# Second FFN of a gated block: activations turned through DRAM, gated values widened by ScalarE, other PSUM banks

## The chip, the cores and the metric

The kernel runs on one core of a Trainium2 chip. A core has TensorE (matmuls and transposes, results in PSUM, eight banks of 2 KB per partition), VectorE, ScalarE and GpSimd for the rest, SyncE that issues transfers, and 16 DMA engines. The engines run side by side, each its own list in order; semaphores are all that ties one list to another. The metric is the device time in microseconds of the whole program.

## The reference

x has 8 batches of 256 rows of 512, that is 16 tiles of 128 rows. Four sublayers are added to x one after the other; the last, the second FFN, is what the change touches:

```python
x = x + tanh(g_xattn[0]) * L0_xattn(ctx, ctx, layernorm(x), ...)
x = x + tanh(g_ffn[0])   * L0_ffn(layernorm(x), ...)
x = x + tanh(g_xattn[1]) * L1_xattn(layernorm(x), ctx, ...)
x = x + tanh(g_ffn[1])   * L1_ffn(layernorm(x), w1, g1, w2, g2, w3, g3)

def _rmsnorm(x, g):  return g * (x * rsqrt(mean(x * x, axis=-1) + 1e-8))
def _act_quant(x):
    scale = 127.0 / clip(max(abs(x), axis=-1), 0.0001)
    return clip(round(x * scale), -128, 127) / scale
def _linear_bit(x, w, g): return _act_quant(_rmsnorm(x, g)) @ _ternary_quant(w).T

def _L1_ffn_ref(x, w1, g1, w2, g2, w3, g3):      # 512 -> 2048 -> 512
    h = silu(_linear_bit(x, w1, g1)) * _linear_bit(x, w2, g2)
    return _linear_bit(h, w3, g3)
```

## The kernel before

A tile t of 128 rows goes through the second FFN in these steps. Its values are small integers after quantisation, kept as bf16.

1. `x_stats` (VectorE, L1685): mean and variance of the row. `x_norm` (GpSimd, L564): four small operations give the factor of LayerNorm and RMS norm together.
2. `x_gain` (VectorE, L1691): (x - mean) * g, once for g1 and once for g2, into `xg`. `x_max`, `x_scales` (L1697, L1701): the largest value and the scales.
3. `x_quant` (ScalarE, L904): int16 into `qi4`. `x_widen` (VectorE, L1711): bf16 into `qb4`.
4. `x_T` (TensorE, L1163): eight 128 by 128 transposes into PSUM bank 2. `x_out` (ScalarE, L922): copy to `xq4T`.
5. `up` (TensorE, L1255): four chunks c of 512 columns. Each is two groups of four matmuls, with w1 into bank 3 + c % 2 and with w2 into bank 5 + c % 2. A chunk waits until `gate` has read the chunk two before it.
6. `silu` (ScalarE, L926) reads the first bank into `sil`, `gate` (VectorE, L1766) multiplies the second bank, its scale and `sil` into `hh`, and counts `h_done`.
7. `h_gain` (GpSimd, L576): hh * g3 into `hg`, 512 columns at a time. `h_max` (VectorE, L1773): the largest of each. `h_squares` (ScalarE, L943): sums of squares over chunks 0 to 2, then 3. `h_rms` (GpSimd, L580) and `h_scales` (VectorE, L1778): the scales.
8. `h_quant` (ScalarE, L931): int16 in two halves. `h_widen` (VectorE, L1790): bf16 into `hqb`, in two halves.
9. `hidden_T` (TensorE, L1264): sixteen transposes into banks 0 and 1. `h_out` (ScalarE, L937): copies to `hqT`.
10. `down` (TensorE, L1272): sixteen matmuls with w3 into bank 7. `finish` (VectorE, L1796): scale and add to `x_res`; SyncE stores the tile (L430).

Every engine has a `ffn_body(t, ...)` in which it does its part of several tiles. In body t, tile t goes through steps 5 to 7 (its scales come in body t+1), tile t-1 through steps 8 to 10, tile t+1 through steps 2 to 4. `finish(t-2)` opens VectorE's body. TensorE's body is `up(t)` chunks 0 to 2, `hidden_T(t-1)`, chunk 3, twelve matmuls of `down(t-1)`, `x_T(t+1)`, the last four. The order within a list is written by hand.

The last two attention bodies (`attn_body(NB - 2)` and `attn_body(NB - 1)`, with NB = 8) prepare tiles 0 and 1, and the end of the last attention batch (`latent_ln(7)`, `relu(7)`, `out_proj(7)`, `attn_end(7)`) lies inside body 0. After body 15 come `finish(14)`, `h_scales(15)`, the widening, `hidden_T(15)`, `down(15)` and `finish(15)`.

## Time and profile before

| | |
|---|---|
| median of 3 runs | 741.81 us (741.56 to 744.07) |
| profiled execution | 739.38 us, its span 737.6 us |
| TensorE matmul, busy over the span | 650.4 us, 88% |
| VectorE | 597.9 us, 81% |
| ScalarE | 493.7 us, 67% |
| GpSimd | 331.7 us, 45% |
| mean granted TensorE clock | 0.970 |
| second FFN, first `up` to the last `finish` | 517.3 to 734.9 us |

Busy time of matmuls runs from start to modelled end of each, and they are pipelined, so it is more than the work. Durations are of one profiled execution. An idle time before an instruction is put down to the engine, or the DMA, whose signal came last. A letter q behind an engine's name (SPq, PEq) means its queue of issues. The span lacks what lies before the first and after the last instruction, 1.8 us here.

### The profile page before, as it was taken

How to read it: one execution, taken by the hardware profiler on the slowest of the kernel's cores; microseconds unless marked ns; L12 is line 12 of the kernel's file. 1: busy time of each engine (PE TensorE's matmuls, PEld its weight loads, DVE VectorE, ACT ScalarE, POOL GpSimd, SP SyncE). 2: the span in 40 equal slices, each digit the busy share in tenths (PEclk: the TensorE clock that was granted, in tenths of full speed). 3: DMA queues.
4: the chain of work that ended last, by engine and by line, in shares of the span. 5: the costliest groups of instructions: out<-in, count | busy, mean ns of one | idle time of the engine just before them, and what ended most of it. 6: DMA issues, size and time to landing. Idle time of an engine off the chain costs nothing.

```text
span 737.6 us, 10458 instructions
## 1 busy us (share of the span) xinstructions
PE 650.4 (88%) x3211; PEld 385.5 (52%) x3211; DVE 597.9 (81%) x1114; ACT 493.7 (67%) x743; POOL 331.7 (45%) x420
## 2 busy tenths in 40 slices
...
DMA packets 73135, 87.38 MB, mean 118 GB/s; under 512 B 36672, under 2 KB 43600, under 8 KB 71952
## 3 DMA queue, kind: packets, MB, share of 16 engines
...
q8 instruction: 14, 0.23, 0.1%
...
## 4 chain that ended last, share of the span: by engine, by line
PE 30%; DVE 22%; issue 22%; ACT 16%; POOL 6%; DMA 3%; DVEq 0%; POOLq 0%; SPq 0%; ACTq 0%
PE ps L1027 16%; PE ps L1133 4%; PE ps L1097 4%; ACT arena L948 4%; DVE arena L1694 3%; DVE q L1699 2%; ACT turn L843 2%; ACT arena L797 2%; DVE arena L1769 2%; ACT turn L908 2%; DMA arena<-kpad_d 1%; DVE arena L1794 1%; PE ps L1278 1%; DMA arena<-in_x 1%; ACT arena L924 1%
## 5 line engine op out<-in xcount | busy, mean ns | idle before, releaser
L1027 PE MATMUL ps<-arena 128*128 128x288 f32 x640 | 159.8, 411 | 6.6 <-POOL arena L492 3.0
L1027 PEld LDWEIGHTS ps<-arena 128*128 128x128 f32 x640 | 121.7, 192 | 41.8 <-issue 7.6
L1260 PE MATMUL ps<-arena 128*128 128x512 bf16 x512 | 116.2, 380 | 9.1 <-ACT arena L924 7.6
L578 POOL TENSOR_TENSOR arena<-arena 128x512 f32<-128x512 f32 x64 | 87.8, 1374 | 68.9 <-DVE arena L1769 68.8
L1260 PEld LDWEIGHTS ps<-arena 128*128 128x128 bf16 x512 | 47.5, 98 | 71.4 <-issue 14.2
L1133 PE MATMUL ps<-arena 128*128 128x512 bf16 x256 | 60.8, 403 | 9.3 <-DVE arena L1583 6.7
L491 POOL TENSOR_TENSOR arena<-arena 128x1024 f32<-128x1024 f32 x32 | 60.6, 1894 | 13.0 <-ACT arena L672 7.5
L1410 DVE TENSOR_TENSOR turn<-ps,arena 128x768 f32<-128x768 f32 x32 | 30.6, 957 | 39.0 <-PE ps L1027 27.2
L1278 PE MATMUL ps<-arena 128*128 128x512 bf16 x256 | 61.9, 387 | 0.1
L1097 PE MATMUL ps<-arena 128*128 128x512 bf16 (+1 forms) x256 | 57.5, 382 | 1.8 <-ACT arena L797 1.7
L498 POOL TENSOR_TENSOR turn<-turn 128x512 f32<-128x512 f32 x32 | 42.5, 1327 | 26.1 <-DVE turn L1420 26.0
L928 ACT ACTIVATE arena<-ps,q 128x512 f32<-128x512 f32 x64 | 41.7, 674 | 16.5 <-PE ps L1260 16.5
L685 ACT ACTIVATE arena<-arena 128x512 f32<-128x512 f32 x32 | 19.9, 626 | 43.9 <-DVE turn L1420 43.9
L1133 PEld LDWEIGHTS ps<-arena 128*128 128x128 bf16 x256 | 26.1, 103 | 43.7 <-issue 17.3
L1769 DVE SCALAR_TENSOR_TENSOR arena<-ps,q,arena 128x512 f32<-128x512 f32 x64 | 47.5, 744 | 0.7 <-ACT arena L928 0.5
L797 ACT ACTIVATE arena<-ps,b,s 128x512 f32<-128x512 f32 x64 | 45.0, 795 | 3.6 <-PE ps L1097 2.7
L1775 DVE TENSOR_REDUCE q<-arena 128x1 f32<-128x512 f32 x64 | 42.0, 676 | 1.7 <-POOL arena L578 1.6
L934 ACT ACTIVATE arena<-arena,q 128x1024 int16<-128x1024 f32 x32 | 35.0, 1141 | 12.3 <-DVE q L1788 12.3
L1504 DVE TENSOR_REDUCE hmax<-arena 128x1 f32<-128x2048 f32 x15 | 34.0, 2277 | 9.2 <-ACT arena L797 9.2
L1097 PEld LDWEIGHTS ps<-arena 128*128 128x128 bf16 x256 | 24.7, 99 | 32.0 <-ACT arena L797 3.1
L1420 DVE TENSOR_TENSOR turn<-ps,turn 128x1024 f32<-128x1024 f32 x32 | 39.2, 1225 | 1.1
L1278 PEld LDWEIGHTS ps<-arena 128*128 128x128 bf16 x256 | 24.8, 99 | 28.2 <-issue 2.4
...
## 6 DMA issues: line engine op xcount, KB each, us to landing
...
tern_d<-late SPq DMA_DIRECT2D x24, 256.0 KB, 6.1
arena<-in_x SPq DMA_DIRECT2D x4, 1024.0 KB, 9.6
arena<-in_ctx SPq DMA_DIRECT2D x4, 1024.0 KB, 17.4
...
x_d<-arena SPq DMA_DIRECT2D x4, 1024.0 KB, 4.2
arena<-x_d SPq DMA_DIRECT2D x4, 1024.0 KB, 7.7
```

Source lines behind the costliest of these rows:

```text
L491: pool.tensor_tensor(dst[:, :, 0:32].rearrange("p r (d i) -> p r d i", d=4), a, shifted, ALU.mult)
L498: po.done(pool.tensor_tensor(x[:, :, 0:16], x[:, :, 0:16], x[:, :, 16:32], ALU.add))
L578: pool.tensor_tensor(hg[:, s, sl], hh[:, s, sl], g3[:, sl], ALU.mult).then_inc(S["hg_done"], 1)
L797: act.activation(hid[:, q, f, :], ps[:, f % 4, :], ACT.Gelu, bias=b1[:, f:f + 1], scale=s1[:, f:f + 1]).then_inc(S["gelu_done"], 1)
L928: act.activation(sil[:, c, :], ps[:, 3 + c % 2, :], ACT.Silu, scale=q4[:, 11 + 2 * s:12 + 2 * s]).then_inc(S["sil_done"], 1)
L1027: last = pe.matmul(ps[:, 4 * s + lo, 0:NB * PAIRS], toep[:, u, (LB - 1 - lo + li) * P:(LB - lo + li) * P], kv[:, s, li, :], start=(li == 0 ...
L1097: last = pe.matmul(ps[:, f % 4, :], fw1T[:, k, f * P:(f + 1) * P], xqT[:, k, ds(L * r, L)], start=(k == 0), stop=(k == LB - 1))
L1133: return pe.matmul(ps[:, 2 * j + f // 8, :], hq[:, r % 2, f, j * P:(j + 1) * P], fw2T[:, f, :], start=(f % 8 == 0), stop=(f % 8 == 7))
L1260: last = pe.matmul(ps[:, 3 + 2 * j + c % 2, :], xq4T[:, s, 4 * j + k, :], w[:, k, c * L:(c + 1) * L], start=(k == 0), stop=(k == LB - 1))
L1278: last = pe.matmul(ps[:, 7, :], hqT[:, f, :], bw3T[:, f, :], start=(f == 0), stop=(f == FT - 1))
L1769: v.scalar_tensor_tensor(out=hh[:, s, c * L:(c + 1) * L], in0=ps[:, 5 + c % 2, :], scalar=q4[:, 12 + 2 * s:13 + 2 * s], in1=sil[:, c, :], ...
L1775: dv.done(v.tensor_reduce(q4[:, 32 + c:33 + c], hg[:, s, c * L:(c + 1) * L], AX, ALU.max, apply_absolute_value=True))
```

## The change

Its parts, by engine:

- SyncE: `x_turned(t)` stores `qb4` (256 KB) to DRAM, waits until it has landed, and reads it back transposed into `xq4T`. `h_turned(t)` does so with `hqb` (512 KB) into `hqT`, which now has two places. Both stand in SyncE's list with the stores of the result: for each t, `h_turned(t-1)`, `store(t-2)`, `x_turned(t+2)`.
- TensorE: `x_T` is gone. `hidden_T` is there for tile 15 alone. `up` writes three pairs of banks, (3, 5), (4, 6), (0, 1) and (3, 5) again; chunk 0 waits for the last gate of the tile before, chunk 3 for the tile's first gate. `down(t-2)` is in body t, in two pieces around `up(t, 3)`, into bank 7 or 2 by turns.
- ScalarE: `x_out` is gone, `h_out` is there for tile 15 alone. It gets `h_widen` (one pass of 2,048 columns after both halves of `h_quant`) and `x_centre` (mean - x into `xc`).
- GpSimd: gets `x_gain`, one product of 1,024 columns of `xc`, repeated, with g1 and g2; for tiles 0 and 1 `x_centre` as well. `h_rms(t-1)`, `x_norm(t+2)` and `x_gain(t+2)` stand before the four `h_gain(t)`.
- VectorE: `x_gain` and `h_widen` are gone, `h_max` works on halves of 1,024 columns. `finish(t-2)` stands between `h_max(t, 0)` and `gate(t, 3)`.
- Tile x is prepared two bodies ahead instead of one.

```diff
@@ SyncE
+            def x_turned(t, s, past):
+                sp.wait_ge(S["qb_ready"], t + 1)
+                if past is not None:
+                    sp.wait_ge(xT_in[s], 16 * past)
+                sp.dma_start(xq_d[s], qb4).then_inc(S["xq_stored"], 16)
+                sp.wait_ge(S["xq_stored"], 16 * t + 16)
+                if past is not None:
+                    sp.wait_ge(S["upb_done"], 4 * t - 4)
+                sp.dma_start_transpose(xq4T[:, s], xq_d[s]).then_inc(xT_in[s], 16)
+            def h_turned(t, s, past):
+                sp.wait_ge(S["hqb_ready"], 2 * t + 2)
+                if past is not None:
+                    sp.wait_ge(hT_in[s], 16 * past)
+                sp.dma_start(hq_d[s], hqb).then_inc(S["hq_stored"], 16)
+                sp.wait_ge(S["hq_stored"], 16 * t + 16)
+                if past is not None:
+                    sp.wait_ge(S["dn_done"], t - 1)
+                sp.dma_start_transpose(hqT[:, s], hq_d[s]).then_inc(hT_in[s], 16)
+            x_turned(0, 0, None)
+            x_turned(1, 1, None)
+            x_turned(2, 0, 1)
+            for t in range(1, NT):
+                h_turned(t - 1, (t - 1) % 2, (t - 1) // 2 or None)
+                if t >= 2:
+                    store(t - 2)
+                if t + 2 < NT:
+                    x_turned(t + 2, t % 2, t // 2 + 1)
@@ GpSimd
+            def x_gain(t):
+                pool.wait_ge(S["xc_ready"], t + 1)
+                pool.tensor_tensor(xg[:, :, :], xc.unsqueeze(1).to_broadcast([P, 2, L]), g12[:, :, :],
+                                   ALU.mult).then_inc(S["xg_ready"], 1)
+            def ffn_body(t, s, nxt2):
+                h_rms(t - 1)
+                if nxt2:
+                    x_norm(t + 2)
+                    x_gain(t + 2)
+                for c in range(4):
+                    h_gain(t, s, c)
+            x_norm(0)
+            x_centre(0)
+            x_gain(0)
             latent_norm(NB - 2)
-            pool.wait_ge(S["gs_in"], 48)
             x_norm(1)
+            x_centre(1)
+            x_gain(1)
+            x_norm(2)
+            x_gain(2)
             latent_norm(NB - 1)
@@ ScalarE
+            def x_centre(t):
+                act.wait_ge(S["st4"], t + 1)
+                act.wait_ge(S["xg_ready"], t)
+                act.activation(xc, x_res[:, ds(t, 1), :].rearrange("p a l -> p (a l)"), ACT.Identity, scale=-1.0,
+                               bias=mv[:, 0, 0:1]).then_inc(S["xc_ready"], 1)
+            def h_widen(t):
+                act.wait_ge(S["hqi3_ready"], 2 * t + 2)
+                if not isinstance(t, int) or t >= 1:
+                    act.wait_ge(S["hq_stored"], 16 * t)
+                act.activation(hqb, hqi, ACT.Copy).then_inc(S["hqb_ready"], 2)
+            def ffn_body(t, s, nxt2, prev):
+                if nxt2:
+                    x_centre(t + 2)
                 silu(t, s, 0)
+                silu(t, s, 1)
                 if prev:
-                    h_quant(t - 1, 1 - s)
-                silu(t, s, 1)
+                    h_quant(t - 1, 1 - s % 2)
                 silu(t, s, 2)
                 if prev:
-                    h_out(t - 1)
-                if nxt:
-                    x_quant(t + 1)
+                    h_widen(t - 1)
+                if nxt2:
+                    x_quant(t + 2)
                 if not prev:
                     relu(NB - 1)
                 silu(t, s, 3)
@@ TensorE
             def up(t, s, chunks):
                 for c in chunks:
-                    pe.wait_ge(S["h_done"], 4 * t + c + 1)
+                    if isinstance(t, int) and t == 0:
+                        if c >= 2:
+                            pe.wait_ge(S["h_done"], c + 1)
+                    elif c == 0:
+                        pe.wait_ge(S["h_done"], 4 * t + 2)
+                    elif c == 2 and isinstance(t, int):
+                        pe.wait_ge(S["x3_done"], 6 + 2 * NB)
+                    elif c == 3:
+                        pe.wait_ge(S["h_done"], 4 * t + 3)
+            def ffn_body(t, s, pair):
+                pe.wait_ge(xT_in[s], 16 * pair + 16)
                 up(t, s, (0, 1, 2))
+                pe.wait_ge(hT_in[s], 16 * pair)
+                down(t - 2, s, 0, 8)
                 up(t, s, (3,))
+                down(t - 2, s, 8, FT)
@@ VectorE
             def attn_body(b, p, nxt, nxt2, prev):
                 if nxt and not nxt2:
-                    v.wait_ge(S["gs_in"], 48)
                     x_stats(0)
-                    x_gain(0)
-                    x_max(0)
+                if not nxt:
+                    x_max(1)
+                    x_scales(1, 1)
+                    x_stats(2)
...
                 if nxt and not nxt2:
+                    x_max(0)
                     x_scales(0, 0)
...
+            def ffn_body(t, s, nxt2, nxt3, prev, prev2):
+                u = s % 2
                 if prev:
+                    h_max(t - 1, 1 - u, 1)
+                    h_scales(t - 1, 1 - u)
                 gate(t, s, 0)
                 gate(t, s, 1)
                 if not prev:
                     latent_ln(NB - 1)
+                if nxt2:
+                    x_max(t + 2)
                 gate(t, s, 2)
+                if nxt2:
+                    x_scales(t + 2, (s + 2) % 4)
+                h_max(t, u, 0)
+                if prev2:
+                    finish(t - 2, u)
                 gate(t, s, 3)
+                if nxt2:
+                    x_widen(t + 2)
                 if not prev:
                     attn_end(NB - 1)
+                if nxt3:
+                    x_stats(t + 3)
```

## Rows read from the trace of the kernel before

**Rows 1.** Busy time of the engines in two stretches of the second FFN.

```profile
core 0: us, PE busy (x) PEld busy (x) DVE busy (x) ACT busy (x) POOL busy (x), PEclk, DMA share, GB/s
544.40:712.30 167.90, 157.92 (x936) 76.28 (x936) 161.99 (x349) 141.06 (x196) 97.09 (x144) 1.00 0.05 20
...
712.30:737.60 25.30, 17.98 (x96) 8.29 (x96) 11.91 (x26) 13.43 (x18) 6.76 (x10) 0.93 0.09 32
```

**Rows 2.** The chain that ended last, bodies 2 to 14, by line.

```profile
by line: issue 20.2%; ACT arena L948 16.0%; DVE arena L1694 12.8%; DVE q L1699 8.8%; DVE arena L1769 6.1%; ACT turn L908 5.8%; DVE arena L1794 4.6%; ACT arena L928 4.4%; POOL q L587 4.3%; ACT arena L924 4.3%; DVE q L1704 1.8%; DVE q L1783 1
```

**Rows 3.** Timeline of bodies 8 and 9: start us, duration us, engine, line, operation.

```profile
624.27 2.19 ACT L934 ACTIVATE arena<-arena,q 128x1024 int16<-128x1024 f32 x2 [0.51 <-DVE q L1788]
...
625.04 1.71 POOL L578 TENSOR_TENSOR arena<-arena 128x512 f32<-128x512 f32 x1 [0.28 <-DVE arena L1769]
...
627.22 0.75 DVE L1794 CAST arena<-arena 128x1024 bf16<-128x1024 int16 x2
...
628.35 1.94 ACT L940 ACTIVATE arena<-ps 128x1024 bf16<-128x1024 bf16 x2 [0.74 <-PE ps L1268]
...
628.68 1.90 PE L1260 MATMUL ps<-arena 128*128 128x512 bf16 x8
...
634.94 5.35 PE L1260 MATMUL ps<-arena 128*128 128x512 bf16 x24 [0.46 <-ACT arena L924]
```

**Rows 4.** Groups of instructions: ns min/median/max, or busy us and mean ns.

```profile
L578 POOL TENSOR_TENSOR arena<-arena x64: 1266/1271/1720, 522.9 to 721.5; 128x512 f32<-128x512 f32 x64
...
L491 POOL TENSOR_TENSOR arena<-arena 128x1024 f32<-128x1024 f32 x32 | 60.6, 1894 | 13.0 <-ACT arena L672 7.5
...
L928 ACT ACTIVATE arena<-ps,q 128x512 f32<-128x512 f32 x52 | 33.7, 673 | 7.8 <-PE ps L1260 7.8
...
L908 ACT ACTIVATE turn<-arena,q 128x512 int16<-128x512 f32 x26 | 17.4, 714 | 3.1 <-DVE q L1709 3.1
...
L948 ACT ACTIVATE arena<-arena 128x512 f32<-128x512 f32 x14 | 8.7, 620 | 0.0
...
L886 ACT ACTIVATE arena<-arena x12 | 23.0, 1916 | 0.0
...
L928 ACT ACT_TABLE_LOAD x1 | 1.3, 1283 | 0.0
...
L1694 DVE SCALAR_TENSOR_TENSOR arena<-arena,mv x32: 740/748/1765, 493.4 to 702.9; 128x512 f32<-128x512 f32 x32
...
L1699 DVE TENSOR_REDUCE q<-arena x16: 1201/1202/1220, 494.9 to 705.9; 128x2 f32<-128x1024 f32 x16
```

**Rows 5.** DMAs: one line's issues and landings, then KB and median landing.

```profile
L416 SPq DMA_TRANSPOSE arena<-tern_d x12: 1972/2365/4210, 368.3 to 398.8; - x12
...
DMA to landing us min/median/max: 4.4/4.9/8.0
...
x_d<-arena SPq DMA_DIRECT2D x4, 1024.0 KB, 4.2
...
out_x<-arena SPq DMA_DIRECT2D x16, 256.0 KB, 2.0
```

**Rows 6.** Timeline of the way into the second FFN.

```profile
508.60 0.19 POOL L551 TENSOR_TENSOR sm<-eps_ln,sm 128x1 f32<-128x1 f32 x1 [13.05 <-DVE sm L1662]
...
515.75 0.70 DVE L1649 BATCH_NORM_STATS2 bn<-ps 128x6 f32<-128x512 f32 x1 [1.96 <-PE ps L1226]
...
527.30 0.74 DVE L1769 SCALAR_TENSOR_TENSOR arena<-ps,q,arena 128x512 f32<-128x512 f32 x1
...
544.45 1.25 PE L1260 MATMUL ps<-arena 128*128 128x512 bf16 x5 [0.52 <-ACT arena L924]
```

**Rows 7.** Timeline of the end.

```profile
720.13 3.62 PE L1278 MATMUL ps<-arena 128*128 128x512 bf16 x16
...
723.79 0.75 DVE L1799 SCALAR_TENSOR_TENSOR arena<-ps,q,arena 128x512 f32<-128x512 f32 x1 [0.26 <-PE ps L1278]
...
728.80 5.31 PE L1278 MATMUL ps<-arena 128*128 128x512 bf16 x16
```

More of the change, by code:

```diff
@@ L219, in flamingo_gated_block @@
         q4 = sb("q4", [P, 36])
+        up_scale = sb("up_scale", [P, 4, 2])
         ps = ctx.enter_context(nc.psum_tensor("ps", [P, 8, 512], F32))
@@ L253, in flamingo_gated_block @@
         c_in = [sem(f"c_in{g}") for g in range(NG)]
+        xT_in = [sem(f"xT_in{s}") for s in range(2)]
+        hT_in = [sem(f"hT_in{s}") for s in range(2)]
         block = ctx.enter_context(nc.Block())
@@ L602, in _ @@
                 h_gain(0, 0, c)
-            h_rms(0)
-            with po.loop(NT // 2 - 1, 10) as i:
+            ffn_body(1, 1, True)
+            with po.loop(NT // 2 - 2, 2 * 5) as i:
                 for u in range(2):
-                    ffn_body(2 * i + 1 + u, (1 + u) % 2, True)
+                    ffn_body(2 * i + 2 + u, u, True)
+            ffn_body(NT - 2, 0, False)
             ffn_body(NT - 1, 1, False)
+            h_rms(NT - 1)
         @block.scalar
@@ L963, in ffn_body @@
                 silu(t, s, 3)
-                h_squares(t, s, 0)
-                if nxt:
-                    x_out(t + 1, 1 - s)
-                h_squares(t, s, 1)
-            x_out(0, 0)
-            ffn_body(0, 0, True, False)
-            with act.Fori(0, NT // 2 - 1) as i:
-                for u in range(2):
-                    ffn_body(2 * i + 1 + u, (1 + u) % 2, True, True)
-            ffn_body(NT - 1, 1, False, True)
+                h_squares(t, s % 2, 0)
+                h_squares(t, s % 2, 1)
+            x_quant(1)
+            ffn_body(0, 0, True, False)
+            ffn_body(1, 1, True, True)
+            with act.Fori(0, 3) as i:
+                for u in range(4):
+                    ffn_body(4 * i + 2 + u, (2 + u) % 4, True, True)
+            ffn_body(NT - 2, 2, False, True)
+            ffn_body(NT - 1, 3, False, True)
             h_quant(NT - 1, 1)
-            h_out(NT - 1)
+            h_widen(NT - 1)
+            h_out()
         @block.tensor
@@ L1160, in _ @@
             pe.wait_ge(S["w3_out"], 1)
-            def x_T(t):
-                pe.wait_ge(S["qb_ready"], t + 1)
-                for n in range(8):
-                    last = pe.transpose(bank_bf(2)[:, n * P:(n + 1) * P], qb4[:, n * P:(n + 1) * P], identb[:, :])
-                last.then_inc(S["xT_tr"], 1)
             def project(b, p):
@@ L1270, in hidden_T, with down @@
                     last.then_inc(S["hT_tr"], 1)
-            def down(t, first, end):
-                if first % 8 == 0:
-                    pe.wait_ge(S["hT_out"], 2 * t + first // 8 + 1)
+            def down(t, s, first, end):
                 if first == 0:
@@ L1685, in x_stats @@
             def x_stats(t):
+                if not isinstance(t, int) or t >= 1:
+                    v.wait_ge(S["xg_ready"], t)
                 dv.done(v.bn_stats(bn[:, 0, :], x_res[:, ds(t, 1), :].rearrange("p a l -> p (a l)")))
```

154 lines of the change are left out of this document (61 added, 93 removed).

## The prediction

> **What bounds the kernel now.** I read the stretches first, then the chain, then one body of the second FFN in order of time. The FFN's 16 tiles take 218 of 737.6 us. From 544.4 (start of body 2) to 712.3 (start of body 15) 13 bodies take 167.9 us, 12.92 each, and VectorE is busy for 161.99/13 = 12.46 of it; TensorE's 12.15 is not its work, since pipelined matmuls count long [rows 1]. Of its real work: 24 matmuls show 5.35 us (634.94) and 8 show 1.90 (628.68) [rows 3], so one costs (5.35 - 1.90)/16 = 0.216 us, and the 48 of a body (32 up, 16 down) 10.35; the last one ends 0.39 after its start. The chain of a body goes through VectorE's `x_gain` (L1694), `x_max`, ScalarE's squares and `x_out` [rows 2]. It closes on itself: tile t+1 is centred, scaled, quantised, turned and projected inside body t.
>
> **VectorE and ScalarE in a body.** VectorE loses `x_gain`, a pair of 0.75 and 1.77 = 2.5 us, and `h_widen`, 0.75; `h_max` becomes two reduces of 1,024 at 1.20 [rows 3, 4]. 12.46 - 3.25 leaves 9.2 busy [rows 1]. ScalarE loses `h_out`, 1.94 [rows 3], and `x_out`, half of that by its form; it gets `h_widen`, the form of L886 (2,048 int16 to bf16), 1.92, and `x_centre`, a 512 pass like the squares' 0.62 [rows 4]: 10.85 - 2.9 + 2.5 = 10.5 busy [rows 1].
>
> **GpSimd in a body.** It gets `x_gain`, 1,024 products. Bounds: 1.89 from L491 (1,024 columns, one operand repeated) and 2.55 from two of L578 [rows 4]. I take 2.4, nearer to L578, whose operands are as large. `h_gain` stays 1.27 and loses its 1.71 case, which lies beside `x_gain` on VectorE [rows 3, 4]. Of its 97.09/13 = 7.47 [rows 1] the four gains are 3 x 1.27 + 1.71 [rows 3, 4], so the norm and root chains 2.0, with their gaps 2.4. The new sum is 5.1 + 2.4 + 2.4 = 9.9.
>
> **The new body.** Time 0 is when TensorE starts `up(t, 0)`. TensorE then has no wait inside the body: `down(t-2)` stands between, and three pairs of banks leave only `up(t, 3)` waiting for `gate(t, 0)`. It ends its 48 matmuls at 10.35. Three loops must be weighed:
> - TensorE and VectorE. VectorE's list is ..., `gate(2)`, `x_scales`, `h_max(0)`, `finish(t-2)`, `gate(t, 3)`. `finish(t-2)` waits for `dn_done`, the last matmul of body t, and `up(t+1, 0)` waits for `gate(t, 3)`. So both lie between two bodies of TensorE. From the last matmul's start: 0.39 to its end, 0.04 to `finish` (723.75 to 723.79), 0.75 for it, the same for the gate, 0.05 to TensorE; less the 0.216 slot already counted [rows 3, 7]. That is 1.77, and the body is 10.35 + 1.77 = 12.1.
> - GpSimd. From the end of `gate(t-1, 3)`: `h_gain` to 1.35, `h_rms` and `x_norm` to 3.75, `x_gain` to 6.15, `h_gain` 0 and 1 to 8.65, then on VectorE `h_max(0)` 1.2, `finish` and `gate` 1.5: 11.4. With 1.89 for `x_gain` it is 10.9, with 2.55 it is 11.5; all hidden. It decides only if GpSimd's part is 0.7 longer.
> - ScalarE. `x_max` ends at 7.3, `gate(2)` 8.0, `x_scales` 8.6, `x_quant` (two of 0.71) 10.0, `silu(3)` (0.67) 10.7, then the gate: 11.4 [rows 4].
>
> I take the first, 12.1. 13 bodies: 167.9 - 157.3 = **10.6 saved**.
>
> **The turns through DRAM.** `h_quant(t-1)` starts at 3.6 (after `silu(1)` and the scales), `h_widen` ends at 8.2. SyncE then waits and issues (0.2), stores 512 KB, waits, and issues the transpose. The store is bounded by 2.0 (256 KB) and 4.2 (1,024 KB), by size 2.7. The transpose of 512 KB landed in 4.4 to 8.0, median 4.9, with up to 12 behind one another [rows 5]. So it lands at 8.2 + 0.2 + 2.7 + 0.1 + 4.5 = 15.7, and `down(t-1)` wants it in the next body at 12.1 + 5.2 = 17.3: 1.6 of cover. If that is gone each us late is a us per body. Behind it on SyncE's queue stand `store(t-2)` and `x_turned(t+2)`; the queue is free again at about 18, the next `hqb` comes at 20.3, and x has 4 us of cover. TensorE is rid of 24 transposes a body, a gain that counts for nothing while it waits 1.77.
>
> **The way in.** `x_centre(1)` and `x_gain(1)` now follow `latent_norm(6)` on GpSimd (508.60 before), and VectorE's `x_max(1)`, `x_scales(1)`, `x_stats(2)` stand before `latent_stats(7)`, which began at 515.75 after an idle 1.96 [rows 6]. Before that, `x_max(0)` behind GpSimd moves the last attention body by 0.8 to 1.4. Then 509.7 + 0.8 + 1.35 + 0.6 + 2.4 = 514.9, and 1.2 + 0.6 + 0.9 give 517.6 for `latent_stats(7)`. In body 0 `x_max(2)` stands before `gate(0, 2)`, and ScalarE's `x_quant(2)` before `relu(7)`, on which `out_proj(7)` hangs: `gate(0, 3)`, begun at 527.30 [rows 6], would end at 532.6 instead of 528.04. `up(1)` has no `down` with it, so half of this comes back. Following body 1 (`attn_end`, four passes at 0.7, statistics 0.9, `h_max`, scales, GpSimd's norm and gain 3.7, `x_max`, gate, scales, reduce, gate), body 2 starts at 546.8 instead of 544.45. I take **+2.4**, between 1.9 and 2.9 by the same steps with the bounds of each.
>
> **The way out.** B is the start of `up(15, 0)`. Before, the last `finish` starts at B + 21.83 (712.33 to 728.80 + 5.31 + 0.04). After, `down(14)` waits for h(14), B + 15.7. TensorE has then been idle 5.4 us; in the last `down` before, after gaps, 16 matmuls took 5.31 instead of 3.62, its first half spaced 0.43 (the 1.2 GHz level; the granted mean of that stretch is 0.93) [rows 1, 7]. So `down(14)` ends at about B + 21.0. h(15): `gate(15, 3)` ends at 12.0, `h_gain` 13.4, `h_max` and scales 15.6, `h_quant` 17.8, `h_widen` in one piece 19.7, so `hidden_T(15)` stands behind `down(14)`: 21.0, then 1.7 to the first half's copy, 3.25 for 15 matmul slots, 0.42 to `finish`: 26.4. **+4.6**; 2.9 if the clock holds in `down(14)`, 5.5 if it doesn't return for `down(15)`.
>
> **Sum.** -10.6 + 2.4 + 4.6 = -3.6 on a span of 737.6. The profiled execution took 739.38 (1.8 around the span), the median 741.81 is 2.4 above that; both are kept. 741.8 - 3.6 = **738.2**. By the bounds: -10.6 + 1.9 + 2.9 = -5.8, and with a body of 12.3, -8.0 + 2.9 + 5.5 = +0.4: its own range is 736.0 to 742.2.
>
> **Rivals.**
> - A, the order costs nothing: TensorE's end and the gate don't form a loop, and GpSimd and ScalarE at 11.4 bind. 13 x 0.7 = 9.1 less: 729.1. For it: nothing but that I may misread a wait. 0.06.
> - B, GpSimd's and VectorE's loop binds: the longest and shortest of L578 (1.27, 1.72) and of L1694 (0.74, 1.77) show [rows 4] that products of two SBUF operands on the two engines disturb each other. For it: only 0.7 of cover and a dozen handovers in that loop. Against: no two-operand SBUF product is left on VectorE in the body. Body 12.6: 13 x 0.5 = +6.5: 744.7. 0.15.
> - C, the slower side: h lands late. It costs from a landing above 6.1 us, and above 6.9 the body is longer than before. At 8.0, the row's maximum: 8.2 + 3.0 + 8.0 - 5.2 = 14.0 per body, +14.2 + 2.4 + 8.1 at the end = +24.7: 766; at 6.9 it is 12.9, and 2.4 + 7.0 for the two ends: 751. Against: the 8.0 had other transposes ahead of it, here at most one of x, with pauses. 0.13.
> - E, the same place at its extreme: the 16 blocks of h are turned one after another. Twelve transposes of 16 blocks each were issued from 368.3 to 398.8, 2.8 us each [rows 5], so a block takes at most 0.17 to 0.28 us of a landing, and this is excluded: 0. By the Trainium skill (VectorE: DVE Perf Modes, The three transpose paths and Rules for kernel authors) a 128 by 128 transpose takes 1309 ns by DMA and 390 on TensorE, which it advises when the result may go to PSUM; sixteen in series would be 20.9 us and a body of about 27, and the trace does not agree that they run in series.
> - D, ScalarE reloads its tables between `x_centre` (Identity) and Silu, 1.28 each, two per body [rows 4]: ScalarE's 10.5 becomes 13.1, and so does the body: 13 x 0.2 + 7.0 = +9.6: 751. No row has the two functions side by side. By the Trainium skill (ScalarE: Activation LUTs, Table sets: the hidden batching unit) identity is in every set, which speaks against it. 0.03.
>
> The forecast keeps 0.63.
>
> **Range and chances.** 0.5% is 3.7 us, about what a measurement can tell here, so the bounds are 738.1 and 745.5. The forecast lies on the first. Faster: 0.32 of the forecast + 0.06 = 0.38. Same: 0.31 + 0.08 of B = 0.39. Slower: 0.07 + 0.13 + 0.03 = 0.23. Range 730 to 750: it leaves out half of A, two thirds of C, and D.
>
> **What would show it.** After the change: body 12.1; on TensorE one gap of 1.8 per body, ended by the gate's line, and VectorE waiting about 0.5 for `down` before `finish`; no wait of TensorE for a DMA in bodies 3 to 15; `x_gain` on GpSimd at 2.4; transposes landing by 5 us; body 2 at 547; 26 us from `up(15, 0)` to the last `finish`, with a gap of 5 before `down(14)`. Wrong if a `down` waits on the DMA, if the gap of TensorE is ended by ScalarE or GpSimd's work, or if `finish` finds `dn_done` already there.

## The result, and the profile after

| | before | after |
|---|---|---|
| median (range) | 742.94 us (741.56 to 745.91) | 757.97 us (755.97 to 760.32), 4 runs each |
| ratio | | 1.0204, 95% interval 1.0168 to 1.0239 |
| profiled execution, its span | 739.38, 737.6 us | 755.97, 754.1 us |
| mean granted TensorE clock | 0.970 | 0.946 |
| x_stats(0) to body 2 | 492.49 to 544.45: 51.96 us | 495.01 to 553.80: 58.79 us |
| bodies 2 to 14 | 167.87 us | 170.64 us |
| up(15, 0) to the last finish | 21.84 us | 26.48 us |

The change made the kernel 15 us slower; 3.6 us faster was forecast. The forecast of the end held (+4.6), the one of the way in was 4.4 too small, and the bodies got 2.8 us longer instead of 10.6 shorter. Another 2.5 us stand ahead of `x_stats(0)`, the first instruction in the table: the profiled executions are 16.6 us apart, and the four stretches are 2.5, 6.8, 2.8 and 4.6. The twelve kernels below have the changed kernel's code up to there; eleven reach `x_stats(0)` at 493.8 to 496.6 and one at 499.8, so it moves by several us without a change of code. How much of the 2.5 belongs to the change stays open.

The stretches that answer [rows 1], in the same columns, and two more that show the clock:

```profile
core 0: us, PE busy (x) PEld busy (x) DVE busy (x) ACT busy (x) POOL busy (x), PEclk, DMA share, GB/s
553.80:724.40 170.60, 144.63 (x611) 61.95 (x624) 135.30 (x265) 135.62 (x181) 118.62 (x151) 0.95 0.48 139
724.40:750.90 26.50, 21.34 (x94) 9.28 (x96) 9.35 (x19) 15.46 (x18) 8.09 (x11) 0.87 0.31 89
...
585.00:632.00 47.00, 38.95 (x176) 17.10 (x177) 38.77 (x73) 39.06 (x51) 33.27 (x40) 1.00 0.47 135
632.30:635.70 3.40, 3.36 (x8) 1.16 (x9) 2.91 (x10) 2.65 (x6) 2.95 (x8) 0.50 1.01 290
```

VectorE did get its relief, 10.4 us busy a body instead of 12.5, and GpSimd is at 9.1 instead of 7.5. Neither is full, and the body is still not shorter. From one `up(t, 0)` to the next the 13 bodies take, in us:

```
13.83 12.71 13.83 12.72 12.73 12.72 13.80 12.72 13.72 12.71 12.71 12.72 13.73
```

There are two lengths. Eight bodies take 12.72. Five take 1.0 to 1.1 more, and each of these has 3.4 us at a granted clock of 0.50, the 1.2 GHz level (in the first it is the second half of a fall of 6.8 us that began before the body). Before, the whole stretch was at 1.00 [rows 1]. Eight times 12.72 and five times 13.8 are the 170.6.

Where 12.72 comes from is read in one body at full clock, the answer to [rows 3]: timeline, start us, duration us, engine, line, operation, and what ended the idle time before it.

```profile
646.14 5.35 PE L1334 MATMUL ps<-arena 128*128 128x512 bf16 x24 [1.61 <-DVE arena L1838]
...
649.87 2.36 POOL L627 TENSOR_TENSOR arena<-turn,arena 128x1024 f32<-128x1024 f32 x1
...
652.20 3.71 POOL L633 TENSOR_TENSOR arena<-arena 128x512 f32<-128x512 f32 x3
652.27 1.22 DVE L1767 TENSOR_REDUCE q<-arena 128x2 f32<-128x1024 f32 x1 [1.20 <-POOL arena L627]
...
653.40 0.74 DVE L1838 SCALAR_TENSOR_TENSOR arena<-ps,up_scale,arena 128x512 f32<-128x512 f32 x1
654.06 0.66 DVE L1772 TENSOR_SCALAR q<-q 128x2 f32<-128x2 f32 x1
...
654.84 1.10 DVE L1775 TENSOR_TENSOR up_scale<-q,ath 128x2 f32<-128x2 f32 x1
655.86 0.21 DVE L1777 TENSOR_SCALAR q<-q 128x2 f32<-128x2 f32 x1
...
656.11 1.33 ACT L972 ACTIVATE turn<-arena,q 128x512 int16<-128x512 f32 x2 [1.82 <-DVE q L1777]
...
657.12 0.73 DVE L1863 SCALAR_TENSOR_TENSOR arena<-ps,q,arena 128x512 f32 x1
657.35 0.67 ACT L994 ACTIVATE arena<-ps,up_scale 128x512 f32<-128x512 f32 x1
...
658.05 0.75 DVE L1838 SCALAR_TENSOR_TENSOR arena<-ps,up_scale,arena 128x512 f32<-128x512 f32 x1 [0.20 <-ACT arena L994]
...
658.86 0.82 PE L1334 MATMUL ps<-arena 128*128 128x512 bf16 x3 [2.19 <-DVE arena L1838]
```

The last row is TensorE's gap, 2.19 us, ended by `gate(3)` (L1838). My forecast of 12.1 would be 1.6 in this column, which counts the last matmul's end too. That gate waits for ScalarE's `silu(3)`, which stands behind `x_quant` (L972), and that waits 1.82 us for `x_scales` (L1772 to L1777). The four instructions of `x_scales` work on two columns. I had 0.6 us for them; they take 2.01, from 654.06 to 656.07. Their product (L1775) takes 1.10 us and ends at 655.94; GpSimd's run of three gains (L633) ends at 655.91. From here on I call this a hold: a VectorE instruction that lasts until GpSimd's running one is over. `finish` (L1863) sits in the wait for `silu(3)` and costs nothing here. Counted from the end of the `gate(3)` before (646.08), `x_max` ends at 7.4 and `gate(2)` at 8.1, where I had 7.3 and 8.0; `x_scales` ends at 10.0 instead of 8.6, and everything behind it keeps that 1.4, up to `gate(3)` at 12.7 instead of 11.4.

The groups of all 16 tiles (ns min/median/max), and the transfers (us min/median/max to landing, of the transpose of h), which answer [rows 4, 5]. The first fence is the product of `x_scales` before the change, 0.14 in every tile:

```profile
L1707 DVE TENSOR_TENSOR q<-q,ath x16: 139/141/144, 499.7 to 707.6; 128x2 f32<-128x2 f32 x16
```

```profile
L1775 DVE TENSOR_TENSOR up_scale<-q,ath x16: 140/1100/1110, 503.0 to 706.7; 128x2 f32<-128x2 f32 x16
...
L1772 DVE TENSOR_SCALAR q<-q x16: 212/588/665, 502.7 to 705.9; 128x2 f32<-128x2 f32 x16
...
L627 POOL TENSOR_TENSOR arena<-turn,arena x16: 2340/2364/2667, 498.2 to 701.7; 128x1024 f32<-128x1024 f32 x16
...
DMA to landing us min/median/max: 4.1/4.4/4.6
```

The way in and the end, for [rows 6, 7]:

```profile
497.90 3.51 DVE L1753 SCALAR_TENSOR_TENSOR arena<-turn,tg,arena 128x512 f32<-128x512 f32 x2
498.20 2.67 POOL L627 TENSOR_TENSOR arena<-turn,arena 128x1024 f32<-128x1024 f32 x1
...
534.73 1.33 ACT L972 ACTIVATE turn<-arena,q 128x512 int16<-128x512 f32 x2 [5.15 <-DVE q L1777]
535.96 0.61 ACT L945 ACTIVATE arena<-arena 128x512 f32<-128x512 f32 x1
...
536.72 3.65 PE L1309 MATMUL ps<-arena,late 128*128 128x512 f32 x4 [5.29 <-ACT arena L945]
...
739.31 6.39 PE L1350 MATMUL ps<-arena 128*128 128x512 bf16 x16 [4.32 <-DMA arena<-hq_d]
```

The residual pair of `attn_end` (L1753), 1.42 us before, takes 3.51 beside GpSimd's `x_gain`, and 3.12 at 523.63 beside the next one. ScalarE's queue holds `relu(7)` (L945) behind `x_quant(2)`, and TensorE stands idle for 5.29 us behind it. The clock took part too: between 504 and 522 us the granted mean is 0.72, and it was 0.91 before.

### The profile page after: what moved, and what is told of

Same layout as the page of the kernel before. It is cut to its first block and busy times, and to the rows that moved or that the text cites. A ratio compares the mean times of both kernels' runs of the same rounds, so it can differ in the third digit from the quotient of the medians.

```text
span 754.1 us, 9475 instructions
## 1 busy us (share of the span) xinstructions
PE 637.4 (85%) x2814; PEld 371.0 (49%) x2843; DVE 569.9 (76%) x1018; ACT 489.4 (65%) x727; POOL 363.6 (48%) x438
## 5 line engine op out<-in xcount | busy, mean ns | idle before, releaser
L1334 PE MATMUL ps<-arena 128*128 128x512 bf16 x503 | 122.5, 399 | 34.0 <-DVE arena L1838 33.6
L633 POOL TENSOR_TENSOR arena<-arena 128x512 f32<-128x512 f32 x64 | 82.4, 1305 | 60.2 <-DVE arena L1838 59.7
L1334 PEld LDWEIGHTS ps<-arena 128*128 128x128 bf16 x512 | 50.8, 102 | 105.3 <-DVE arena L1838 41.0
L1208 PE MATMUL ps<-arena 128*128 128x512 bf16 x251 | 60.4, 403 | 9.8 <-DVE arena L1655 6.9
L1350 PE MATMUL ps<-arena 128*128 128x512 bf16 x248 | 62.5, 393 | 5.4 <-DMA arena<-hq_d 4.3
L1838 DVE SCALAR_TENSOR_TENSOR arena<-ps,up_scale,arena 128x512 f32<-128x512 f32 x64 | 46.8, 746 | 14.6 <-ACT arena L994 9.0
L994 ACT ACTIVATE arena<-ps,up_scale 128x512 f32<-128x512 f32 x64 | 43.1, 675 | 17.6 <-PE ps L1334 17.6
L1208 PEld LDWEIGHTS ps<-arena 128*128 128x128 bf16 x256 | 26.2, 103 | 43.7 <-issue 17.0
L1845 DVE TENSOR_REDUCE q<-arena 128x1 f32<-128x1024 f32 x32 | 38.8, 1212 | 8.1 <-POOL arena L633 8.1
L1350 PEld LDWEIGHTS ps<-arena 128*128 128x128 bf16 x256 | 25.6, 101 | 37.5 <-DMA arena<-hq_d 4.8
L1172 PEld LDWEIGHTS ps<-arena 128*128 128x128 bf16 x256 | 24.8, 99 | 31.8 <-ACT arena L861 3.2
L972 ACT ACTIVATE turn<-arena,q 128x512 int16<-128x512 f32 x32 | 21.3, 714 | 27.9 <-DVE q L1777 27.9
```

The source lines that it names most:

```text
L633: pool.tensor_tensor(hg[:, s, sl], hh[:, s, sl], g3[:, sl], ALU.mult).then_inc(S["hg_done"], 1)
L994: act.activation(sil[:, c, :], ps[:, up_banks(t, c)[0], :], ACT.Silu, scale=up_scale[:, s, 0:1]).then_inc(S["sil_done"], 1)
L1172: last = pe.matmul(ps[:, f % 4, :], fw1T[:, k, f * P:(f + 1) * P], xqT[:, k, ds(L * r, L)], start=(k == 0), stop=(k == LB - 1))
L1208: return pe.matmul(ps[:, 2 * j + f // 8, :], hq[:, r % 2, f, j * P:(j + 1) * P], fw2T[:, f, :], start=(f % 8 == 0), stop=(f % 8 == 7))
L1334: last = pe.matmul(ps[:, bank, :], xq4T[:, s, 4 * j + k, :], w[:, k, c * L:(c + 1) * L], start=(k == 0), stop=(k == LB - 1))
L1350: last = pe.matmul(ps[:, 7 if s == 0 else 2, :], hqT[:, s, f, :], bw3T[:, f, :], start=(f == 0), stop=(f == FT - 1))
```

## The experiments

All are edits of the changed kernel. The ratio is to the kernel before on the same chip, whose medians were 742.57 (first four), 743.08 (next four) and 741.87 (last four). Body is the median of bodies 2 to 14, `2 to 14` their sum; end is from up(15, 0) to the last finish. These three columns are of the profiled execution, the median is of all. e9 to e12 ran on another chip than e1 to e8.

| kernel | median us (range) | ratio, 95% interval | body | 2 to 14 | end |
|---|---|---|---|---|---|
| after | 757.97 (755.97 to 760.32) | 1.0204 (1.0168 to 1.0239) | 12.72 | 170.64 | 26.48 |
| e1_product_late | 753.86 (749.41 to 754.83) | 1.0155 (1.0084 to 1.0226) | 12.58 | 168.00 | 26.51 |
| e2_columns_apart | 754.96 (752.54 to 757.38) | 1.0198 (1.0127 to 1.0269) | 12.60 | 169.81 | 25.62 |
| e3_finish_last | 751.69 (749.66 to 755.63) | 1.0137 (1.0071 to 1.0202) | 12.79 | 166.24 | 25.74 |
| e4_filler | 748.52 (746.30 to 750.82) | 1.0101 (1.0032 to 1.0170) | 12.71 | 165.83 | 25.45 |
| e5_gains_wait | 743.57 (740.69 to 746.65) | 1.0001 (0.9969 to 1.0033) | 12.15 | 160.04 | 26.14 |
| e6_way_in | 751.67 (748.63 to 753.09) | 1.0120 (1.0060 to 1.0181) | 12.71 | 170.84 | 26.86 |
| e7_tail | 751.03 (748.46 to 752.80) | 1.0114 (1.0054 to 1.0174) | 12.73 | 170.75 | 22.80 |
| e8_all | 734.29 (731.95 to 739.64) | 0.9898 (0.9866 to 0.9931) | 11.89 | 154.91 | 24.08 |
| e9_store_twice | 752.78 (748.90 to 755.17) | 1.0152 (1.0094 to 1.0210) | 12.55 | 165.96 | 27.85 |
| e10_no_filler | 730.71 (725.43 to 734.63) | 0.9849 (0.9780 to 0.9917) | 11.91 | 153.91 | 22.78 |
| e11_gain_on_vector | 775.54 (770.87 to 776.48) | 1.0447 (1.0389 to 1.0505) | 14.67 | 189.64 | 25.26 |
| e12_widen_last | 729.83 (728.77 to 731.86) | 0.9847 (0.9802 to 0.9892) | 11.82 | 153.35 | 22.78 |

**Is it this product, or any short instruction?** e1 takes the product out of `x_scales` and makes it just before `finish`.

```diff
 def x_scales(t, s):
-    v.tensor_tensor(up_scale[:, s, :], q4[:, 7:9], ath[:, 0:2], ALU.mult)
 def ffn_body(...):
     h_max(t, u, 0)
+    x_up_scale((s + 2) % 4)
```

> The two-column product into up_scale (0.14 us where GpSimd is idle, 1.10 in the bodies after the change, where it ends each time within 0.05 us of the end of a GpSimd h_gain) leaves x_scales and stands right before finish, when GpSimd is idle. Theory P (a VectorE instruction with two SBUF tensor operands is held until GpSimd's running instruction ends; the one-operand scalings are held less or not): x_scales falls from 2.0 to 0.9 us, the loop GpSimd - x_max - gate - x_scales - x_quant - silu - gate of 12.72 to about 11.7, and the loop down - finish - gate - up binds at 12.1: a body at the full clock takes 12.1, 13 x 0.6 = 8 us less in all. Rival Q (every small VectorE instruction between SBUF columns is held to the next GpSimd boundary, and only the number of boundaries counts): the last scaling now waits for the boundary that the product waited for, the body stays at 12.7, the time within 2 us of the changed kernel's. Rival R (ScalarE or the transfers set 12.72): no change either, and the product itself still 1.1 or not as it may.

The timeline of one body of e1:

```profile
614.21 3.73 POOL L633 TENSOR_TENSOR arena<-arena 128x512 f32<-128x512 f32 x3
...
616.09 0.66 DVE L1772 TENSOR_SCALAR q<-q 128x2 f32<-128x2 f32 x1
...
616.98 0.99 DVE L1776 TENSOR_SCALAR q<-q 128x2 f32<-128x2 f32 x1
...
619.02 0.14 DVE L1779 TENSOR_TENSOR up_scale<-q,ath 128x2 f32<-128x2 f32 x1
```

The product falls to 0.14, but the last scaling, which took 0.22 in its old place, takes 0.99 and ends at 617.97, 0.03 after the gains (617.94). The hold moved to the next instruction, and the body lost 0.14, as rival Q had it. The median fell by 4.1, more than the 2 that Q allowed; the bodies' sum gives 2.6 of it. e2 has e1's edit, and the columns of `x_max` and `x_scales` lie two words apart:

```diff
+qx = sb("qx", [P, 4, 2])
-v.tensor_scalar(q4[:, 9:11], q4[:, 5:7], q4[:, 4:5], -QMAX, ...)
+v.tensor_scalar(qx[:, 0:2, 1], qx[:, 0:2, 0], q4[:, 4:5], -QMAX, ...)
```

> As e1, and the columns of x_max and x_scales lie two words apart instead of side by side. Theory S (the two small scalings are held only because their columns lie densely, so that VectorE takes the path that it shares with GpSimd): both take 0.22 beside GpSimd, x_scales is 0.6 long, the loop through ScalarE shrinks to 11.4 and the body is 12.1 by the loop down - finish - gate - up. Rival Q (density doesn't matter): the scalings are still stretched to GpSimd's boundaries, 0.5 to 1.1 for one of them, and the body is as in e1.

```profile
601.11 0.66 DVE L1774 TENSOR_SCALAR qx<-qx,q 128x2 f32<-128x2 f32 x1
...
602.00 0.99 DVE L1778 TENSOR_SCALAR qx<-qx,q 128x2 f32<-128x2 f32 x1
```

In e2's timeline the same 0.66 and 0.99 stand, and the body is 12.60: how the columns lie makes no difference.

**Does the prediction's loop bind?** e3 puts `finish(t-2)` behind `gate(t, 3)`, which opens that loop.

```diff
-if prev2: finish(t - 2, u)
 gate(t, s, 3)
+if prev2: finish(t - 2, u)
```

> finish(t-2) stands behind gate(t, 3) instead of ahead of it, nothing else. The prediction's theory (the loop down - finish - gate - up sets the body): TensorE's gap falls by finish's 0.75 and the body at the full clock from 12.72 to about 12.0. Theory P (the loop through GpSimd and the held x_scales sets it, and finish fits in while VectorE waits for silu(3)): the body stays at 12.7, the time within 1.5 us of the changed kernel's.

The start of a body with a fallen clock in e3, behind one at full clock, and the start of the next:

```profile
610.22 7.04 PE L1334 MATMUL ps<-arena 128*128 128x512 bf16 x24 [2.25 <-DVE arena L1838]
...
623.11 1.25 PE L1334 MATMUL ps<-arena 128*128 128x512 bf16 x5 [0.67 <-DVE arena L1838]
```

The body at full clock is 12.79, no shorter, so there the loop does not set it. In the slow bodies it does. At a granted clock of 0.50 TensorE needs 1.7 us more (7.04 for 24 matmuls instead of 5.35), and its own end becomes the late one. In the changed kernel the gap behind such a body is 1.6, the length that I had forecast (it is ahead of the body shown above, in its first row), and `finish` waits 1.0 to 2.5 for `down` in these five bodies and in none of the eight others. With `finish` out of the way that gap is 0.67, and a slow body takes 12.9 (13.2 the first, 12.0 the last) instead of 13.7 to 13.8; there are four of them. The sum over the bodies fell by 4.4 and the median by 6.3, where "within 1.5" was expected: the expectation had the body right and left out the slow ones.

**What lets the clock fall?** e4 adds eight matmuls without use to the end of each body of TensorE.

```diff
 down(t - 2, s, 8, FT)
+pe.wait_ge(S["h_done"], 4 * t + 4)
+for f in range(8):
+    pe.matmul(ps[:, 4, :], bw1T[:, 0, 0:P], bw2T[:, 0, 0:L], start=True, stop=True)
```

> Eight matmuls of weights on weights (1.73 us) into bank 4, which nobody reads before it is written again, at the end of each TensorE body from 2 on, in the gap of 2.19 us. They add nothing to what is computed. Theory T (the clock falls to its 1.2 GHz level because TensorE stands idle in each body, and each fall makes a body of 12.72 one of 13.8): no half-rate stretch is left in bodies 3 to 14, all take 12.7 to 12.8, about 5 us less. Rival U (the falls don't hang on the gaps of the bodies): five or so of 13 bodies still take 13.8, and the time is the changed kernel's or more.

```profile
553.80:700.00 146.20, 141.10 (x632) 62.24 (x643) 121.80 (x240) 120.49 (x162) 107.73 (x142) 0.99 0.50 145
```

That is the stretch of e4's bodies: the granted clock is 0.99 instead of 0.95, the length at full clock is the same 12.71, and no body after the first is longer. TensorE's waiting is what differs: 0.45 us a body in its timeline instead of 2.19. The first fall stays; it begins at 549.4, ahead of the bodies that have the filler. So the four later falls come with the gaps, and the sum is 4.8 us smaller without them. The median fell by 9.4, the profiled execution by 7.0; the rest of it lies outside the bodies.

**Without the hold.** e5 leaves VectorE as it is and keeps GpSimd's third gain back until `x_scales` is through.

```diff
 for c in range(4):
+    if nxt2 and c == 2:
+        pool.wait_ge(S["qs_ready"], t + 3)
     h_gain(t, s, c)
```

> Edit: before its third gain of a tile GpSimd waits until x_scales(t+2) is done; nothing else. Theory Q (short VectorE instructions of x_scales are held until GpSimd's running gain ends): only the first of the four can still be held (up to about 654.67 in the trace's body 10), no gain runs beside the others, so x_scales shrinks from 2.0 to about 1.1 us, the product takes 0.14, ScalarE's x_quant starts 0.8 earlier and the full-clock body falls from 12.72 to 12.1, where the loop of my prediction (last down matmul, finish, gate(3), up: 10.35 + 1.77) would bind; 13 bodies lose 0.6 x 13 = 7.8 us, so about 750. Rival (the loss is not the hold but GpSimd's own length): the wait adds to GpSimd's list, and the body stays at 12.7 or grows to 13.2, and the time is 758 or more.

A body of e5:

```profile
640.15 5.35 PE L1338 MATMUL ps<-arena 128*128 128x512 bf16 x24 [1.61 <-DVE arena L1842]
...
646.20 2.50 POOL L633 TENSOR_TENSOR arena<-arena 128x512 f32<-128x512 f32 x2
...
648.07 0.66 DVE L1776 TENSOR_SCALAR q<-q 128x2 f32<-128x2 f32 x1
...
648.85 0.14 DVE L1779 TENSOR_TENSOR up_scale<-q,ath 128x2 f32<-128x2 f32 x1
648.97 0.23 DVE L1781 TENSOR_SCALAR q<-q 128x2 f32<-128x2 f32 x1
...
650.83 0.75 DVE L1867 SCALAR_TENSOR_TENSOR arena<-ps,q,arena 128x512 f32 x1 [0.52 <-PE ps L1354]
```

One wait more on an engine made the kernel 14 us faster; 10.6 of it is in the bodies' sum. `x_scales` takes 1.13, the product 0.14, and only the first instruction is still held to the end of a gain (648.73 against 648.70). The body is 12.15 and later 12.04, `finish` waits 0.52 for `down`, and after body 2 the clock does not fall. This is the body that I had forecast for the change, with the loop that I had forecast.

**The way in.** e6 gives the gains of tiles 0 and 1 back to VectorE and puts `relu(7)` ahead of `x_quant(2)`.

```diff
 def x_max(t):
+    if isinstance(t, int) and t <= 1:
+        x_gain(t)
     v.wait_ge(S["xg_ready"], t + 1)
...
 x_norm(0)
-x_centre(0)
-x_gain(0)
 latent_norm(NB - 2)
...
-if nxt2:
-    x_quant(t + 2)
 if not prev:
     relu(NB - 1)
+if nxt2:
+    x_quant(t + 2)
```

> Edit: x_gain of tiles 0 and 1 is done by VectorE in two products, as before the change, right before x_max; x_quant(2) moves behind relu(7) on ScalarE. Theory Q: the residual pair of attention's end then takes 1.42 us instead of 3.51 in the tile 0 case (the second pair, at 523.6, still stands beside x_gain(2)); latent_stats(7), at 521.08 after the change, starts 2 to 3 us earlier; with relu(7) starting when its input is there (531.4 instead of 536.0), body 2 starts at about 550 instead of 553.8, and the time is 3 to 5 us less than the changed kernel's 758. Rival (the way in is set by where x_max(1) stands in VectorE's list, whoever makes the gain): latent_stats(7) moves by less than 1 us and the time by less than 2.

```profile
496.82 1.42 DVE L1746 SCALAR_TENSOR_TENSOR arena<-turn,tg,arena 128x512 f32<-128x512 f32 x2
...
512.56 6.69 PE L1284 MATMUL ps<-arena 128*128 128x512 f32 x8 [3.08 <-DVE arena L1733]
...
528.51 0.63 ACT L938 ACTIVATE arena<-arena 128x512 f32<-128x512 f32 x1 [1.86 <-DVE arena L1733]
```

The pair (L1746) is back at 1.42. From `x_stats(0)` to body 2 it is 54.86 us instead of 58.79: 3.9 gained, as expected, but only 0.7 of it at `latent_stats(7)` (25.4 instead of 26.1 after `x_stats(0)`; 2 to 3 was expected), which now waits for TensorE's 8 matmuls, 6.69 us here, 6.35 after the change and 5.40 before it. `relu(7)` (L938) starts 9.2 us after it, instead of 14.9 after the change and 9.0 before. So most of what came back stood at `x_quant(2)`, a step that my sum had, with a hold of 1 us ahead of it that it had not. The two edits were made together, so their shares are read from the trace and not from runs of their own. The profiled execution fell by 4.5, 1.1 of it ahead of the changed lines, the median by 6.3.

**The end.** e7 turns the last two tiles' h on TensorE, and VectorE widens the last one in halves.

```diff
-pe.wait_ge(hT_in[0], 16 * (NT // 2))
+hidden_T(NT - 2)
+pe.wait_ge(S["hT_out"], 2)
 down(NT - 2, 0, 0, FT)
```

> Edit: the last two tiles' quantised values are turned by TensorE instead of through DRAM; for the last tile VectorE widens them in two halves as before the change. Theory (the transfer and the widening in one piece cost the 4.4 us at the end): down(14) starts at about up(15,0) + 13.5 instead of + 14.9 to 15.7, TensorE's gap before it shrinks from 4.3 to about 1 us, and the last finish comes 22.5 us after up(15,0) starts instead of 26.5: 4 us less in all, about 754. Rival: the end is set by gate(15,3), the gains and h_scales(15), then only the widening counts and the gain is under 2 us.

```profile
735.98 3.63 PE L1352 MATMUL ps<-arena 128*128 128x512 bf16 x16 [1.21 <-DVE arena L1903]
```

`down(14)` comes 12.6 us after `up(15, 0)` (723.35), with 1.21 of idle ahead of it, and takes 3.63 instead of 6.39; the last finish is at + 22.80, where 22.5 was expected. The profiled execution fell by 4.8 where 4 was expected, 1.2 of it ahead of the changed lines; the median fell by 6.9.

**All of it.** e8 has the edits of e3, e5, e6 and e7 and six filler matmuls.

> Edit: the edits of e5 (GpSimd's wait), e6 (way in) and e7 (end), with finish(t-2) behind gate(t,3) and six filler matmuls at the end of each body. Theory Q with the clock theory: bodies of 11.7 to 12.1 at full clock and no fall of the clock in them: 13 x 12.0 = 156 for bodies 2 to 14 instead of 170.6; with 4 us at the way in and 4 at the end the time is 758 - 14.6 - 8 = 735, below the kernel before's 742. Rival (another handover, about as long as those removed, takes over): bodies of 12.5 and more, 742 or above.

It came out at 734.29, below the kernel before, where 735 was expected, with bodies of 11.7 to 12.0 at full clock. e10 is e8 without the filler:

> Edit: e8 without the filler matmuls. Clock theory (falls come with gaps of 2.2 us per body and not with 1.8, as in e5, nor less): no fall of the clock inside bodies 3 to 14, the body stays at 11.9, and the time is within 2 us of e8's 734.3. Rival (six matmuls per body are what holds the clock up at this body length): some bodies are 1 us longer at a granted clock of 0.5, and the time is 738 or more.

The bodies are the same, 11.89 in e8 and 11.91 here, and no fall of the clock comes back after body 2. Gaps of 1.4 to 1.6 us need no filler here. It had cost 1.3 us at the end (24.08 against 22.78) and 1.3 in body 14, which prepares no x and in which it hides behind nothing (11.67 against 10.37). The time is 3.6 below e8's, where "within 2" was expected.

**How much cover has the transfer?** e9 is e5 with the store of h made twice.

```diff
 sp.dma_start(hq_d[s], hqb).then_inc(S["hq_stored"], 16)
+sp.wait_ge(S["hq_stored"], 32 * t + 16)
+sp.dma_start(hq_d[s], hqb).then_inc(S["hq_stored"], 16)
```

> Edit: the kernel of e5, and the store of each tile's h to DRAM is made twice, one after the other, before its transpose. In e5's trace the transpose of h(t-1) is issued at 638.80 and lands 4.4 us later, 643.2; down wants it at 645.1: cover 1.9 us. A second store adds about 2.6. Theory (lateness beyond the cover is paid once per body, as rival C priced it): the body grows by 2.6 - 1.9 = 0.7 us, from 12.15 to about 12.8, TensorE waits for that DMA in most bodies, and the time is 743.6 + 9 + 2.6 (end) = 755. Rival (the transfers overlap with what else is waited for, or the landing isn't what down waits for): body still 12.1, time below 748.

TensorE's waits (line waited for: us in total, times, longest us) and one body of e9:

```profile
PE ps L1356 <- DMA arena<-hq_d: 10.4, 11, 6.4
```

```profile
641.39 0.33 SPq L458 DMA_DIRECT2D hq_d<-arena  x1
...
644.02 1.32 SPq L462 DMA_TRANSPOSE arena<-hq_d  x1
...
648.45 1.90 PE L1356 MATMUL ps<-arena 128*128 128x512 bf16 x8 [0.26 <-DMA arena<-hq_d]
```

The second store delays the transpose by 2.63 us (641.39 to 644.02), and the body grows by 0.40; TensorE's waits for it are 0.4 each, (10.4 - 6.4) / 10, the 6.4 being at the end of the kernel. What comes late is paid once a body, as rival C had it. By that the cover in e5 was 2.2 us, where its trace gave 1.9; the size rests on this one delay. The body was expected at 12.8 and the time at 755.

**The other direction.** e11 keeps the change but leaves `x_gain` on VectorE for all tiles.

```diff
-pool.tensor_tensor(xg[:, :, :], xc.unsqueeze(1).to_broadcast([P, 2, L]), g12[:, :, :], ALU.mult)
+v.scalar_tensor_tensor(out=xg[:, j, :], in0=..., scalar=mv[:, 0, 0:1], in1=g12[:, j, :], ...)
```

> Edit: the changed kernel with one part undone: x_gain of all tiles is done by VectorE in two products right before x_max, GpSimd's x_gain and x_centre are gone. VectorE gets 0.75 to 1.77 us for each product (rows 4), 2.5 per tile, GpSimd loses 2.4. Theory Q: GpSimd's gains still run beside x_scales and now also beside x_gain, so VectorE's list is 10.4 + 2.5 + about 2 of holds = about 14.5 us at most and 13 at least per body; the time is 760 to 775. Rival (GpSimd's load is the matter: with 2.4 us less on it the gains end before x_scales): x_scales falls to 0.7 us, the body to 12.3 or less, and the time to 750.

```profile
647.99 2.42 DVE L1762 SCALAR_TENSOR_TENSOR arena<-arena,mv 128x512 f32<-128x512 f32 x2
648.15 1.71 POOL L633 TENSOR_TENSOR arena<-arena 128x512 f32<-128x512 f32 x1 [1.47 <-DVE arena L1837]
...
652.40 1.27 POOL L633 TENSOR_TENSOR arena<-arena 128x512 f32<-128x512 f32 x1 [2.54 <-DVE arena L1837]
...
652.57 1.11 DVE L1774 TENSOR_TENSOR up_scale<-q,ath 128x2 f32<-128x2 f32 x1
```

775.54 us, a body of 14.67, both just above what was expected (760 to 775, 13 to 14.5); the granted clock falls in most bodies here, behind gaps of 2.5 to 3.6 us, which the expectation left out. The hold works both ways: the pair takes 2.42 instead of 1.41 and the gain beside it 1.71 instead of 1.27, and the product is held as before (1.11, ending with the gain of 652.40). Less load on GpSimd does not help where the two still meet.

**One more hold.** In e10's order (shown from e8) `x_widen` meets the fourth gain; e12 puts `x_stats(t+3)` ahead of it.

```diff
-x_widen(t + 2)
 x_stats(t + 3)
+x_widen(t + 2)
```

> Edit: e10 with x_stats(t+3) before x_widen(t+2) on VectorE. In e8's trace x_widen takes 1.06 us instead of 0.42 because it ends with GpSimd's gain (644.13 to 645.19, gain to 644.91), x_stats ends 1.1 us later for it, and GpSimd's x_norm (646.17) and all behind it (x_gain, x_max, gate(2), x_scales) wait for it. Theory Q: statistics are not held, st4 comes 1.0 us earlier, the body falls from 11.9 to 11.2 to 11.4, and the time by about 7 us, to 727. Rival (the chain through GpSimd is not what closes the loop now): the body stays at 11.8 to 11.9, and the time at 734.

First e8, then e12:

```profile
643.63 1.28 POOL L631 TENSOR_TENSOR arena<-arena 128x512 f32<-128x512 f32 x1 [1.36 <-DVE arena L1852]
644.13 1.06 DVE L1797 CAST turn<-turn 128x1024 bf16<-128x1024 int16 x1
```

```profile
634.13 0.43 DVE L1794 CAST turn<-turn 128x1024 bf16<-128x1024 int16 x1
...
636.50 2.37 POOL L625 TENSOR_TENSOR arena<-turn,arena 128x1024 f32<-128x1024 f32 x1
```

The cast is back from 1.06 to 0.43, and yet the body fell only from 11.91 to 11.82, where 11.2 to 11.4 was expected, and the time 727. I had not followed GpSimd's own list: gate(3) ends at 632.73 in e12, and gain, root and norm run with hardly a pause until `x_gain` starts at 636.50, 3.8 later (3.9 in e8). So `st4` was late by hardly more than the list itself. The median of 729.83 is not to be told from e10's 730.71. These two are the fastest versions, 1.5% under the kernel before.

## Why the prediction was wrong

- **The body, 12.1.** The step that failed is the term `x_scales` = 0.6 in ScalarE's loop (8.0 to 8.6 in its list). It measured 2.0, and with it that loop came from 11.4 to 12.7, over the 12.1 that I took. The sign that I had named for being wrong was there: `finish` found `dn_done` already there, in the eight bodies at full clock. The reason stood in rival B as a sentence that is false: "no two-operand SBUF product is left on VectorE in the body". One is left, of two columns; I had looked for large ones. With the term put right (e5) the body is 12.15 to 12.04 and the loop that I had named sets it.
- **Rival B had the mechanism, not its place or size.** It priced 0.5 us in the loop of GpSimd and VectorE. It was 0.62, through `x_quant` and `silu(3)` on ScalarE. By the Trainium skill (SBUF — State Buffer, Who interferes with whom) VectorE's second SBUF port pair is GpSimd's only one and is locked for a whole instruction, by whichever starts first; it is taken by products with two SBUF inputs and by copies, casts and `tensor_scalar` in a two-port mode, not by reduces. The traces agree: the product (1.10) and the scalings (0.66, 0.99) end within 0.05 us of GpSimd's instruction, the cast (1.06) and the pair (3.51) 0.3 and 0.5 behind it, and elsewhere they take 0.14, 0.22, 0.42 and 1.42; the reduces stay at 1.2 and the gates, whose one input is in PSUM, at 0.75. Read for instructions of every size, this rule would have pointed at `x_scales`.
- **The clock.** I had no term for it in the bodies; the prediction put it at nothing without a reason. TensorE at 158 of 168 us before never fell [rows 1]; with 2.2 us of waiting in 12.7 it was down in five bodies of 13. In e5, at the forecast body, it was down in the first alone.
- **The bodies' sum.** Between the forecast 157.3 and 170.6 lie 13.3 us. Body 14 prepares no x: without a fall it takes 12.1 (e4), so `x_scales` costs 12 x 0.62 = 7.4, and 5.9 are left for the clock, 4.8 for the four falls that e4 took away and 1.1 for the first.
- **The way in, +2.4.** It was +6.8. I had moved the instructions and left their durations: the pairs of `attn_end` came to 3.51 and 3.12 instead of 1.42, and `x_scales(2)` has a hold of 1 us ahead of `x_quant(2)`, with `relu(7)` behind it and TensorE at half clock (granted 0.50 from 536.7 to 540.1) after its wait (3.65 for the four matmuls of `out_proj(7)`, 1.88 for those of `out_proj(6)`). "Half of this comes back" was wrong too: counted from `x_stats(0)`, `gate(0, 3)` ended 7.4 us later than before the change, and body 2 still started 6.8 later. e6 gave back 3.9 of the 6.8; what the rest is made of was not tested.
- **The way out, +4.6.** Right: 26.48 from up(15, 0), forecast 26.4. In it `down(14)` started at + 14.9, not 15.7, and took 6.39, not 5.3.
- **The transfers.** Right: landing at 4.4 (4.5 forecast), no wait of TensorE for them in the bodies, cover 2.2 by e5 and e9 (1.6 forecast). Rival A falls with e5, where `finish` waits for `down`. Rivals C and E fall, and D too: the only table load of the stage is the one that was there before.
- **GpSimd's gain.** 2.36, forecast 2.4; moving it was right in its cost and wrong in its neighbours.
